# Output products of a mixture-of-experts stage as three split passes, with second weights loaded and split per tile, and a last routing group with records of its own

## What is computed

```python
x = layernorm(x + local_attention(x))          # 8 heads of 128, windows of 128
scores = softmax(x @ gate_w.T)                 # 8 experts
weights, idx = top_k(scores, 2)
h = einsum('td,eid->eti', x, w1)               # 512 -> 256 for each expert
g = silu(h) * einsum('td,eid->eti', x, w3)
eo = einsum('eti,edi->etd', g, w2)             # 256 -> 512
y = sum over the two chosen experts of weight * eo
z = silu(x @ ws1.T) * (x @ ws3.T) @ ws2.T      # one shared expert
x = layernorm(x + y + z)
```

## Time and profile before

| | |
|---|---|
| median of 3 runs | 1709.22 us (1704.3 to 1712.07) |
| the profiled execution | 1706.91 us |
| its span | 1705.2 us |
| busy, share of the span | PE 95%, PE weight loads 79%, DVE 51%, ACT 38%, POOL 38% |
| moved by DMA | 128.76 MB |

### The profile page before, as it was taken

How to read it: one execution, slowest core, us unless ns; L and a number is a source line. 1 busy time by engine, 2 the same in 40 slices (tenths; PEclk the granted TensorE clock), 3 DMA queues, 4 the chain that set the end, 5 groups by cost and what they waited for, 6 DMA issues and landing times.

```text
span 1705.2 us, 30983 instructions
## 1 busy us (share of the span) xinstructions
PE 1627.0 (95%) x9466; PEld 1353.7 (79%) x9467; DVE 868.3 (51%) x2363; ACT 643.6 (38%) x1544; POOL 648.1 (38%) x724
## 2 busy tenths in 40 slices
PE   6899999999999999999999999859999999999986
PEld 4898899899889989988998999846677777677653
DVE  5355655655655656556556556536222222222687
ACT  4233333433343343333334333434233333333333
POOL 3222333343243243334333432522444444443443
PEclk9799999999999999999999999989999999999999
DMA  8010100100000010001001000437233333233785
GB/s 292 1 44 26 32 20 19 37 19 19 25 31 19 18 37 18 19 25 31 19 19 37 19 19 25 148 87 231 87 104 105 99 104 103 100 105 115 265 301 201
DMA packets 75099, 128.76 MB, mean 76 GB/s; under 512 B 9688, under 2 KB 26584, under 8 KB 75056
## 3 DMA queue, kind: packets, MB, share of 16 engines
q1 hardware_dynamic: 55584, 81.54, 14.2%
q0 software_dynamic: 13696, 38.24, 6.9%
q10 hardware_dynamic: 5776, 8.43, 1.9%
HBM read 88.98 MB, written 39.20 MB: 75 GB/s over the span
## 4 chain that ended last, share of the span: by engine, by line
PE 56%; issue 26%; POOL 8%; DVE 5%; DMA 2%; ACT 2%; POOLq 0%; ACTq 0%; DVEq 0%; SPq 0%
PE bank L1105 17%; PE bank L1034 14%; PE bank L1061 9%; PE bank L1176 6%; POOL rnorm L648 3%; PE bank L1195 2%; PE bank L1008 2%; POOL slot_d L633 2%; PE bank L1163 2%; PE bank L1150 1%; DVE qkn L1349 1%; PE bank L1044 1%; POOL pp L654 1%; POOL ga L740 1%; DVE ssum L1337 1%
## 5 line engine op out<-in xcount | busy, mean ns | idle before, releaser
L1105 PE MATMUL bank<-wh,xh 128*128 128x512 f32 (+2 forms) x896 | 339.1, 378 | 10.4 <-DVE qkn L1349 5.0
L1105 PE MATMUL bank<-wl,xh 128*128 128x512 f32 (+2 forms) x896 | 327.9, 366 | 0.0
L1105 PE MATMUL bank<-wh,xl 128*128 128x512 f32 (+2 forms) x896 | 327.6, 366 | 0.0
L648 POOL TENSOR_TENSOR rnorm<-ssmax,nhalf 128x4 f32<-128x4 f32 x128 | 134.0, 1047 | 422.3 <-DVE ssmax L1342 419.1
L1105 PEld LDWEIGHTS bank<-wh,xh 128*128 128x128 f32 x896 | 170.3, 190 | 43.0 <-DVE qkn L1349 16.7
L1105 PEld LDWEIGHTS bank<-wh,xl 128*128 128x128 f32 x896 | 170.0, 190 | 28.5
L1105 PEld LDWEIGHTS bank<-wl,xh 128*128 128x128 f32 x896 | 170.5, 190 | 22.8
L1349 DVE TENSOR_TENSOR qkn<-bank,rnorm 128x512 f32<-128x512 f32 x128 | 88.5, 692 | 132.0 <-POOL rnorm L648 132.0
L1328 DVE TENSOR_TENSOR bl<-bank,bh 128x512 fp32r<-128x512 f32 x104 | 71.7, 690 | 164.2 <-ACT bh L803 164.2
L1195 PE MATMUL bank<-woh,oh 128*128 128x256 f32 (+1 forms) x512 | 147.5, 288 | 1.0 <-DVE xr L1414 1.0
L1195 PE MATMUL bank<-wol,oh 128*128 128x256 f32 (+1 forms) x512 | 144.8, 283 | 0.0
(11 more groups left out here) (197 smaller groups left out, 3481.1 us busy)
## 6 DMA issues: line engine op xcount, KB each, us to landing
xt<-in_xT SPq DMA_DIRECT2D x33, 256.0 KB, 3.2
xr<-in_x SPq DMA_DIRECT2D x32, 256.0 KB, 2.6
x_d<-xr SPq DMA_DIRECT2D x32, 256.0 KB, 2.1
bx<-x_d SPq DMA_DIRECT2D x32, 256.0 KB, 4.1
ga<-eo_d SPq DMA_DIRECT2D x16, 512.0 KB, 4.8
gb<-eo_d SPq DMA_DIRECT2D x16, 512.0 KB, 6.2
out<-oo SPq DMA_DIRECT2D x32, 256.0 KB, 2.6
passing<-in_wqkvT SPq DMA_DIRECT2D x4, 1024.0 KB, 16.3
```

Source lines behind the costliest of these rows:

```text
L648: pool.tensor_tensor(rnorm[:, :], ssmax[:, :], nhalf[:, :], ALU.pow).then_inc(rn_s, 1)
L1105: mm = pe.matmul(b[:, 0:n], a[:, par, c, :], wt[:, c, cols], start=(c == 0 and k == 0), stop=(c == DC - 1 and k == 2))
```

## The change

1. The output product becomes three split passes: the turned hidden values are kept as `gTh` (ACT) and `gTl` (DVE, new function `turned_low`), the weights as a high and a low part.
2. The second weights of an expert tile are loaded in its step from SP's queue (`load_second`) into one of two buffers `w2_raw`, split by ACT into `w2h` and by DVE into `w2l` (`second_low`). The eight loads of `w2e` go away. The shared expert's second weights are split once (`shared_second`, `sh2l`).
3. The last routing group writes records and slots of its own (`rec_last`, `slot_last`), and its `route_choose` has no wait for the scatter ahead. POOL's `weight_low(0)` moves to step 5.
4. At attention's end `heads_low(u, 1)` goes ahead of `mask_max(u, 0)` on DVE, and the token transposes of tiles 0 and 1 ahead of `scores(u, 1)` on TensorE.

```diff
@@ sync @@
+            def load_second(q, q0):
+                b = q0 % 2
+                if q0 >= S1 + 2:
+                    sp.wait_ge(w2_lo, row(q, q0) - 1)
+                    settled(sp)
+                e = nc.values_load(expert_of[0:1, bass.ds(row(q, q0), 1)], ...)
+                sp.dma_start(w2_raw[:, b, :, :],
+                             w2T[bass.ds(e, 1), :, :].rearrange("a (c p) n -> p (a c) n", p=P)).then_inc(w2_in[b], 16)
...
+                if q0 + 1 == S1:
+                    sp.wait_ge(experts_s, 1)
+                if kind(q0 + 1) == "ex":
+                    load_second(q + 1, q0 + 1)
@@ gpsimd @@
             scatter_records(NG - 2, range(G))
-            weight_low(0)
-            next_ids(NG - 2)
             scatter_records(NG - 1, range(G))
...
-                if q0 in (SLOT_Q, SLOT_Q + 1):
-                    weight_low(q0 - SLOT_Q + 6)
+                if q0 in (5, SLOT_Q, SLOT_Q + 1):
+                    weight_low(max(0, q0 - SLOT_Q + 6) if q0 > 5 else 0)
@@ scalar @@
-                act.activation(gT[:, par, :, :], bank[4 + par][:, 0:I], ACT.Copy).then_inc(gt_s, 1)
+                act.activation(gTh[:, par, :, :], bank[4 + par][:, 0:I], ACT.Copy).then_inc(gt_s, 1)
+            def shared_second():
+                act.wait_ge(sh2_in, 16)
+                act.activation(sh2h[:, :, :], sh2_raw[:, :, :], ACT.Copy).then_inc(sh2_hi, 1)
...
-                if 5 <= q0 < 9:
-                    for e in (2 * q0 - 10, 2 * q0 - 9):
-                        act.dma_start(w2e[:, e, :, :], w2T[e, :, :].rearrange("(c p) n -> p c n", p=P))\
-                           .then_inc(w2_in, 16)
+                if kind(q0) == "ex":
+                    act.wait_ge(w2_in[par], 8 * (row(q, q0) - par) + 16)
+                    if q0 >= S1 + 2:
+                        act.wait_ge(eo_s, q - 1)
+                    act.activation(w2h[:, par, :, :], w2_raw[:, par, :, :], ACT.Copy).then_inc(w2_hi, 1)
@@ tensor @@
             def expert_out(q, q0):
-                pe.wait_ge(gt_s, q + 1)
+                pe.wait_ge(gt_lo, q + 1)
...
-                    w2 = w2e[:, bass.ds(expert_at(row(q, q0)), 1), :, :].rearrange("p a c n -> p (a c) n")
+                    pe.wait_ge(w2_lo, row(q, q0) + 1)
+                    hi, lo = w2h[:, par, :, :], w2l[:, par, :, :]
...
-                    mm = pe.matmul(bank[6 + par][:, :], gT[:, par, m, :], w2[:, m, :], start=(m == 0), stop=(m == IC - 1))
+                    for k, (a, b) in enumerate(((gTh, hi), (gTh, lo), (gTl, hi))):
+                        mm = pe.matmul(bank[6 + par][:, :], a[:, par, m, :], b[:, m, :], start=(m == 0 and k == 0),
+                                       stop=(m == IC - 1 and k == 2))
...
-            scores(u, 1, False)
             turn_tokens(0, 0)
             pe.wait_ge(res_s, 2 * u - 1)
             turn_tokens(1, 1)
+            scores(u, 1, False)
@@ vector @@
+            def turned_low(q, q0):
+                dve.wait_ge(gt_s, q + 1)
...
+                dve.tensor_tensor(gTl[...], bank[4 + par][:, 0:I], gTh[...], ALU.subtract).then_inc(gt_lo, 1)
+            def second_low(q, q0):
+                dve.wait_ge(w2_hi, row(q, q0) + 1)
+                dve.tensor_tensor(w2l[...], w2_raw[...], w2h[...], ALU.subtract).then_inc(w2_lo, 1)
...
+            turned_low(0, 0)
             split_b(3, 3)
+            turned_low(1, 1)
             gate_hidden(2, 2)
             add_residual(0, 0)
             add_residual(1, 1)
-            route_choose(NG - 1)
+            route_choose(NG - 1, last=True)
...
                 if q0 + 1 < NQ:
                     split_b(q + 1, q0 + 1)
+                turned_low(q - 1, q0 - 1)
...
                     gate_hidden(q, q0)
+                if kind(q0) == "ex":
+                    second_low(q, q0)
```

More of the change, by code:

```diff
@@ L189, in block_kernel @@
         gg = sbuf(sb, "gg", [P, 2, I])
-        gT = sbuf(sb, "gT", [P, 2, IC, P])
-        sh2 = sbuf(sb, "sh2", [P, IC, GRP])
+        gTh = sbuf(sb, "gTh", [P, 2, IC, P], F32R)
+        sh2h = sbuf(sb, "sh2h", [P, IC, GRP], F32R)
         eo = sbuf(sb, "eo", [P, 2, D])
-        w2e = sbuf(sb, "w2e", [P, E, IC, GRP])
+        s2 = ExitStack()
+        sh2_raw = sbuf(s2, "sh2_raw", [P, IC, GRP])
+        s2.close()
+        sh2l = sbuf(sb, "sh2l", [P, IC, GRP], F32R)
+        w2_raw = sbuf(sb, "w2_raw", [P, 2, IC, GRP])
+        w2h = sbuf(sb, "w2h", [P, 2, IC, GRP], F32R)
+        w2l = sbuf(sb, "w2l", [P, 2, IC, GRP], F32R)
+        sbuf(sb, "to_the_tables", [P, IC, GRP])
         jx = sbuf(sb, "jx", [P, NX, E])
@@ L210, in block_kernel @@
         sh13l = sbuf(sb, "sh13l", [P, DC, GRP], F32R)
-        sbuf(sb, "to_the_end_of_xr", [P, 2, DG])
+        gTl = sbuf(sb, "gTl", [P, 2, IC, P], F32R)
+        sbuf(sb, "to_the_end_of_xr", [P, 2 * DG - 2 * IC * P])
         bx2 = sbuf(sb, "bx2", [P, 1, D])
@@ L289, in block_kernel @@
         sh2_in = sem("sh2_in")
-        w2_in = sem("w2_in")
+        sh2_hi = sem("sh2_hi")
+        sh2_lo = sem("sh2_lo")
+        w2_in = [sem(f"w2_in{i}") for i in range(2)]
+        w2_hi = sem("w2_hi")
+        w2_lo = sem("w2_lo")
+        gt_lo = sem("gt_lo")
         bx_in = [sem(f"bx_in{i}") for i in range(5)]
@@ L626, in scatter_records @@
             def scatter_records(g, tiles):
+                last = isinstance(g, int) and g == NG - 1
+                slots, records = (slot_last, rec_last) if last else (slot_u, rec)
                 pool.wait_ge(rt, slots_at(g))
-                pool.wait_ge(rec_id, g + 1)
+                if not last:
+                    pool.wait_ge(rec_id, g + 1)
                 settled(pool)
@@ L633, in scatter_records @@
                         pool.indirect_dma_start(out=slot_d,
[L634 to L635 removed]
+                                                out_offset=bass.IndirectOffsetOnAxis(slots[:, k, t:t + 1], 0),
+                                                in_=records[:, t, k, :], in_offset=None).then_inc(scat, 16)
             def next_ids(g):
@@ L1483, in route_shift, with route_choose @@
                 chained(dve.tensor_tensor(shifted[:, :, :], logits[:, :, :], per_tile(r_m[:, :]), ALU.subtract), g - 1, n + 1)
-            def route_choose(g, first=False):
+            def route_choose(g, first=False, last=False):
                 if first:
-                    dve.wait_ge(route_const, 6)
-                else:
+                    dve.wait_ge(route_const, 7)
+                elif not last:
                     dve.wait_ge(scat, 32 * G * g)
+                records = rec_last if last else rec
                 dve.wait_ge(rt_exp, g + 1)
@@ L1603, in _ @@
             row_stats(u - 1, 0, False)
+            heads_low(u, 1, u % 2, False)
             mask_max(u, 0, u % 2, False)
-            heads_low(u, 1, u % 2, False)
             finish_rows(u - 1, 0, 0)
```

48 lines of the change are left out of this document (33 added, 15 removed).

## The result

The changed kernel takes 1757.43 us (median of 4 runs, 1755.87 to 1759.8), the kernel before 1708.74 beside it: ratio 1.0293, 95% interval 1.0271 to 1.0314. It is slower, as forecast, but by 49 us where 26 were forecast, and outside the range. The profiled execution took 1759.8 us with a span of 1758.0.

The account below looks back on a forecast made before the run. TensorE alone was taken to set the pace in the expert stretch before the change. From the profiled 1706.9 us, + 41 - 15 - 1 + 3.5 - 1 gave 1734.4, stated as 1735 us, with a range of 1718 to 1752.

Parts of the forecast that it names:

- Ring: Expert tiles: the chain eo, w2h, w2l, bl, gTl, output product sets a period of 5.71 us, adding 41 us.
- Loads: Expert tiles: 72 second-weight loads of 512 KB, one per step, stay hidden behind other work, cost 0.
- Last routing group: Steps ahead of the experts: choosing without the wait for the scatter saves 15.0 us, bounds -18 and -7.
- I take 31: the gain stands at -15: From the output product behind the choosing to step 9: 31 us against 31.2 before, so the 15 us gain is kept.
- two POOL weight splits, all unchanged: 0: From step 9 to the first expert product: slot contents, three gathers and two POOL splits stay as before, cost 0.
- Rival 2: Steps 3 to 8: transfers bunch, bx lands late, head gain is 3 instead of 15, total 1747 us; chance 0.15.
- Rival 3: Expert tiles: POOL's result scatter holds w2l on DVE, 0.9 us more a tile, +64, total 1799 us; chance 0.03.
- Tail: After the experts: three shared tiles at TensorE's pace, -1; combine steps 6.63 instead of 6.39 us, +3.5.
- End of attention: Reordering heads_low ahead of mask_max and token transposes ahead of scores: -1 us, bounds -2 and +1.
- Rival 1: Expert tiles: the ring is hidden, TensorE's period 4.78 us holds, total 1668 us; chance 0.05 faster, 0.05 same.

Follow-up runs that it names:

- half_w2l: The changed kernel with DVE computing only the first half of w2l for each expert tile but the first two; 1717.4 us, ratio 1.0080.
- small_loads: The changed kernel with all but the first two loads of expert second weights moving 32 KB instead of 512 KB; 1758.2 us, ratio 1.0308.
- pool_writes_only: The changed kernel with POOL's three w13 low-part splits replaced by zero fills that read no SBUF; 1751.6 us, ratio 1.0273.
- dve_splits: The changed kernel with all eight w13 low parts on DVE, ahead of the residual in steps 4 to 11, none on POOL; 1746.7 us, ratio 1.0255.
- routing_only: The kernel before with only the last routing group's own records and slots added, products still in float32; 1694.6 us, ratio 0.9937.
- four_eo: The changed kernel with four instead of two result buffers for the shared tiles; 1753.1 us, ratio 1.0280.
- all_mended: The changed kernel with w2h made earlier on ACT, four shared-tile result buffers and all w13 low parts on DVE; 1687.0 us, ratio 0.9888.

## Why the prediction was right in sign and short in size

The spans differ by 52.8 us (1758.0 to 1705.2); the prediction's terms add to 27.5. Term by term:

- **Ring, forecast +41, measured +48.2.** The mechanism is shown from three sides: the rows, w2h moved, w2l halved. The terms add up to 5.71 and half the periods are 5.68. The others are 5.91, so the mean is 5.78 and not 5.71: 0.07 over 70 periods, 5 us. The first period is 8.5 (its w2h waits 2.8 us for its load): 3 us more. The term was mis-sized by these two. Why gTl to the product takes 0.65 in two of four periods I could not settle; the same pattern stands in `half_w2l` (5.14 and 5.38).
- **Loads, forecast 0, measured 0 in the loop,** shown by `small_loads` for the 70 loads that it shrinks. The first two come late: w2h waits 1.4 and 2.8 us for them, the second of which is in the ring's figure.
- **Last routing group, forecast -15.0 at the end of the first output product behind it, and -15 kept up to the experts; measured -1.2 to the first expert `eo`.** This is the step that failed. Its first half held within 3 us: the product behind the choosing began at 1135.58, where I had 1133.4, and ended at 1137.2, where I had 1134.8. I had put the first two output products at full speed, to end at 1128.4; TensorE had stood 2.48 us before them, the granted clock in 1126 to 1129.5 was 0.57, and they ended at 1130.7. But the next residual waits for the store of a tile two back, which the prediction did not look at. The second half, "I take 31: the gain stands at -15" and "two POOL weight splits, all unchanged: 0", took the durations of the DVE splits from the kernel before. They hold there because DVE's split began first and POOL's had to wait. In the changed kernel DVE's split stands behind a residual that stands behind a product that stands behind gTl, while POOL's moved: step 5 instead of the scatters, and behind the slot table's fetch. POOL's began first, twice. `pool_writes_only` and `dve_splits` take POOL's splits away, with DVE's in their old place and in a new one, and the head falls by 11.3 and 13.9. By ratio the second gains 0.38 points, some 6.5 us (its interval just touches that of the changed kernel); I take the cause as shown, by the rows above all, and the size as known only to 7 to 14.
- **The store's wait** is real in the rows (6.84 us on TensorE), but alone it is worth only 6.5 in the head and 0.13 points by ratio, and nothing that can be measured once the clash is gone: token rows are late next.
- **Rival 2** named a swallowed gain of 12 of 15 at 0.15, by late token rows. The size was right and the cause another; with the split products in the shared tiles, late rows come forward only once the clash is mended. In `routing_only` they do at once (8.36).
- **Rival 3** had the right mechanism and the wrong victim: I asked whether POOL's issuing would hold w2l, and did not ask it of the splits of w13, although shows the lock at work. The Trainium skill, page "SBUF — State Buffer", section on two separate sides, says that of such a pair the one that starts first keeps the port for its whole instruction and the other fully blocks. The two pairs of after and the pair of `routing_only` agree (2.15 and 2.16 us from POOL's end to DVE's, and 5.83 on POOL); the first pairs in `four_eo` and `small_loads` do not by their records, since DVE's row starts 0.48 and 0.17 ahead of POOL's and it was still DVE that was held.
- **Tail, forecast -1 + 3.5, measured +5.3.** In the ten kernels with split shared products it is 131.6 to 133.7, in the kernel before and the three experiments without them 124.2 to 127.2. So the cause named, gTl in the shared tiles' path, is the right one and was mis-sized by 3. The combine steps came as forecast, 6.66 apart for 6.63, with `nm` down from 1.40 to 0.15. What the sum left out are two other steps, the third shared one behind the experts and one amid the combine steps: 6.75 and 6.66, where the kernel before has 5.13 and 5.15.
- **End of attention, forecast -1, measured +0.5 at the last `xr`.** But after was already 1.6 us late at 1090, ahead of the edit, so 1.1 were won behind it. That fits the forecast; a shift of that size can't be told from scatter.
- **Rival 1** decided nothing here. With the ring out of the way its 4.78 is the period of most tiles, and 4.94 the mean.

## What to carry to other kernels

Follow the new instruction on its engine to whatever released the instruction ahead of it: a copy that waits for nothing itself is on the path when it is queued behind one that does, and moving it ahead of that one was worth 62 us in the experts' stretch, 57 in all. A gain at one place changes which of two engines begins first where one can hold the other, so durations from the old trace hold only for the old order; wherever a row shows one engine stretched by the other, give the other outcome as a case with its price. And where two parts of a change touch, time each alone: here the routing part was worth 11 us by itself, and the split product cost 48 us in the experts' stretch, where with the ring out of the way it wins 14.

## What the runs showed of the hardware that was not expected

The order of starts in the records did not settle who was held: in `four_eo` DVE's split has its row from 1154.96 and POOL's from 1155.44, DVE took 7.22 and ended 2.15 after POOL's end. DVE's row began while POOL was issuing the slot table's fetch (1154.41 to 1155.41), 0.55 after that issue's start. `small_loads` has the same: DVE's row from 1160.65, 0.86 into the issue and 0.17 ahead of POOL's split, took 6.92. In the earlier trace rows a DVE split that began within such an issue, 0.16 after its start, was not held, and POOL's split behind the issue was. What decides between these cases the runs do not show. POOL's issues are themselves stretched by a DVE split that begins ahead of them; in `all_mended`, the issue of the first gather, for which 1.02 is usual, lasted until 0.89 after the split:

```profile
1175.78 2.28 DVE L1370 TENSOR_TENSOR w13l<-w_f,w13h 128x2048 fp32r<-128x2048 f32 x1
1175.89 3.06 POOL L760 DMA_INDIRECT bx<-x_d,idxc  x1 [0.88 <-POOL idxc L757]
```
